# A state-space layer with two layer norms on one core: the states' product goes ahead of the transposes in pass B

## The reference

```python
xn    = layernorm(x) * gamma + beta
delta = sigmoid(xn @ w_delta + b_delta)        # 16 states
B     = xn @ w_in + b_in
gate  = sigmoid(xn @ w_gate + b_gate)          # 512 x 512
h_t   = tanh((h_{t-1} * delta_t) @ A + B_t)    # scan over 2048 tokens
x     = layernorm(x + (h @ C) * gate + x)
x     = layernorm(x + real(ifft(fft(x) @ w)) + bias)   # w complex, 512 x 512
```

## Time and profile before

| | |
|---|---|
| median of 3 executions | 883.58 us |
| the profiled execution | 883.95 us, its span 882.2 us |
| PE busy | 845.7 us, 96% |
| DVE busy | 744.0 us, 84% |
| POOL busy | 573.6 us, 65% |
| ACT busy | 558.6 us, 63% |
| granted TensorE clock | 0.996 of full, mean |

### The profile page before, as it was taken

How to read it: one execution, slowest core, us unless ns; L and a number is a source line. 1 busy time by engine, 2 the same in 40 slices (tenths; PEclk the granted TensorE clock), 3 DMA queues, 4 the chain that set the end, 5 groups by cost and what they waited for, 6 DMA issues and landing times.

```text
span 882.2 us, 16544 instructions
## 1 busy us (share of the span) xinstructions
PE 845.7 (96%) x5062; PEld 453.8 (51%) x5094; DVE 744.0 (84%) x1507; ACT 558.6 (63%) x1060; POOL 573.6 (65%) x906
## 2 busy tenths in 40 slices
PE   8889999999889999999999999999999999999996
PEld 5445445454444555554455555554555555555553
DVE  7788888889999889888789999888888888888883
ACT  5244444544444444454368888888888888888887
POOL 4565566687755465656756767676777777777772
PEclk9999999999999999999999999999999999999999
DMA  8388888777665656877556575767868766866843
GB/s 309 144 288 303 312 303 320 256 262 271 211 220 197 233 183 233 295 243 246 204 175 213 194 237 192 236 223 245 255 239 259 244 234 236 271 221 223 276 152 143
DMA packets 94190, 209.52 MB, mean 238 GB/s; under 512 B 3761, under 2 KB 5041, under 8 KB 90161
## 3 DMA queue, kind: packets, MB, share of 16 engines
q1 hardware_dynamic: 93840, 208.49, 69.0%
q10 hardware_dynamic: 288, 0.27, 0.2%
HBM read 139.53 MB, written 67.11 MB: 234 GB/s over the span
## 4 chain that ended last, share of the span: by engine, by line
PE 56%; DVE 13%; issue 11%; POOL 10%; DMA 5%; ACT 4%; another core or an unknown queue 0%; POOLq 0%; DVEq 0%; SPq 0%; ACTq 0%
PE bank L1508 15%; PE bank L1509 14%; PE bank L1511 14%; PE bank L1479 5%; POOL lo_sb L798 5%; DMA x_sb<-x 5%; DVE bn L1224 3%; PE bank L1664 2%; PE bank L1591 2%; DVE xs_sb L1256 2%; DVE gsum_sb L1271 2%; PE bank L1571 1%; ACT hi_sb L557 1%; DVE zh_sb L1140 1%; DMA w_ring<-w_gate 1%
## 5 line engine op out<-in xcount | busy, mean ns | idle before, releaser
L798 POOL TENSOR_TENSOR lo_sb<-xs_sb,hi_sb 128x512 f16<-128x512 f32 x128 | 150.0, 1172 | 147.1 <-ACT hi_sb L557 147.1
L1508 PE MATMUL bank<-wg_hi,hi_sb 128*128 128x512 f16 x508 | 192.8, 380 | 7.5 <-DVE gsum_sb L1271 6.1
L877 POOL TENSOR_TENSOR x_sb<-x_sb,gate_sb 128x512 f32<-128x512 f32 x120 | 152.9, 1275 | 70.8 <-DMA x_sb<-x 66.6
L1508 PE MATMUL bank<-w_re_sb,hi_sb 128*128 128x512 f16 x512 | 194.0, 379 | 1.5 <-DVE w_ring L1382 1.5
L1509 PE MATMUL bank<-w_re_sb,hi_sb 128*128 128x512 f16 x512 | 194.0, 379 | 0.0
L1509 PE MATMUL bank<-wg_lo,hi_sb 128*128 128x512 f16 x508 | 192.6, 379 | 0.0
L557 ACT ACTIVATE hi_sb<-xs_sb 128x512 f16<-128x512 f32 x128 | 80.5, 629 | 173.5 <-DVE xs_sb L1256 171.1
L1261 DVE SCALAR_TENSOR_TENSOR lo_sb<-bank,hi_sb 128x512 f16<-128x512 f32 x128 | 88.5, 692 | 55.6 <-ACT hi_sb L717 54.0
L1511 PE MATMUL bank<-w_re_sb,lo_sb 128*128 128x512 f16 x512 | 131.4, 379 | 0.0
L1511 PE MATMUL bank<-wg_hi,lo_sb 128*128 128x512 f16 x508 | 131.3, 381 | 0.0
L725 ACT ACTIVATE norm_sb<-x_sb,lift_bias,rstd 128x512 f32<-128x512 f32 x128 | 103.1, 806 | 14.3 <-POOL lift_bias L890 14.1
(11 more groups left out here) (198 smaller groups left out, 1351.7 us busy)
## 6 DMA issues: line engine op xcount, KB each, us to landing
x_sb<-x SPq DMA_DIRECT2D x63, 1024.0 KB, 6.4
gate_dram<-gate_sb SPq DMA_DIRECT2D x32, 1024.0 KB, 5.2
out<-out_sb SPq DMA_DIRECT2D x31, 1024.0 KB, 5.4
gate_sb<-gate_dram SPq DMA_DIRECT2D x30, 1024.0 KB, 7.1
out_sb<-x_turned SPq DMA_DIRECT2D x16, 1024.0 KB, 7.4
norm_sb<-x_turned SPq DMA_DIRECT2D x15, 1024.0 KB, 7.3
w_ring<-gate_dram SPq DMA_DIRECT2D x2, 1024.0 KB, 9.6
x_sb<-x SPq DMA_DIRECT2D x2, 512.0 KB, 6.2
```

The costliest lines, as they stand in the source:

```text
L798: pool.tensor_tensor(lo_sb[:, k % 4], xs_sb[:, k % 2], hi_sb[:, k % 4], ALU.subtract).then_inc(s_lo, 1)
L877: pool.tensor_tensor(x_sb[:, k // 4, k % 4], x_sb[:, k // 4, k % 4], gate_tile(n, k), ALU.add).then_inc(s_v, 1)
L1508: nc.tensor.matmul(dst, hi_sb[:, slot_of, t], w_hi[:, t], start=(t == 0), stop=False)
```

## The change

In `slot_b` of TensorE the states' product of tile n + 7 is issued ahead of the transposes of tile n + 1, behind the scan's step. Nothing else differs.

```diff
             def slot_b(n, k, v):
                 scan_slot(1, n)
+                if exists(n + 7):
+                    states_out(n + 7, (k + 7) % 8, v if k < 1 else v + 1)
                 if exists(n + 1):
                     transpose(n + 1, k + 1, s_bnorm, s_bhi, s_blo, s_bt)
-                if exists(n + 7):
-                    states_out(n + 7, (k + 7) % 8, v if k < 1 else v + 1)
                 if exists(n):
                     ffn(n, k)
                 check_slot(1, n)
```

## The result

The changed kernel takes 888.09 us (median of 6 executions, 886.76 to 889.11), the kernel before 883.66 us (6 executions beside them, 882.09 to 884.31). The ratio is 1.0047, 95% interval 1.0035 to 1.0058: **slower by 4.2 us** (the two medians lie 4.4 apart), where 1.9 were forecast, and outside the range. A second set of 6 gave 1.0040 (1.0025 to 1.0055).

The account below looks back on a forecast made before the run. PE's own instructions were taken to set the pace. Terms 0.6 - 0.5 + 0.7 + 0.5 + 0.5 gave +1.8 us, 1.9 unrounded, so 885.5 us against a median of 883.58; range 882.5 to 887.8.

Parts of the forecast that it names:

- quiet slots keep 3.24 us: Some 85 of 128 slots where nothing waits: PE's own work stays 3.24 us a slot, cost 0.
- new waits for `gated`: Sign: in slots 40, 42, 44 and 46 the states' product newly waits for `gated`.
- `ffn_sum` would cost more: Sign: PE's waits for `ffn_sum` grow from 1.5 us in five places to over 2 in more.
- Both rivals on the low side: Product fills the waits for the normalisation, 882.5 us, chance 0.17; shift taken up everywhere, within 0.5 of 883.6, chance 0.12.
- the ring of 3.24 us: Rival: loop from `gated` through states' product and transposes back becomes the bound, +11, 894 us, chance 0.06.
- the forecast's own case: The summed terms hold: time between 883.8 and 887.4 us, chance 0.65.
- Slot 0, +0.6: Slot 0: twelve products start 0.65 us later, 0.07 comes back in slot 2; bounds 0.5 to 0.7.
- Scan's spacing, -0.5: Slots 5 to 33: transposes' first load is hidden behind the states' product, 0.017 us a slot; bounds -0.5 and 0.
- Scan's VectorE, +0.7: Slots 6, 12 and 20: POOL's residual sums move by 0.22 us, delaying VectorE's product and `ffn_sum`; bounds 0 and 0.9.
- The split, +0.5: Slots 38 to 46: states' high half later, VectorE's low half ends after POOL's sum, which moves 0.22 us; bounds 0.2 and 1.4.
- the bound of 1.4: Upper bound for slots 38 to 46: VectorE's low half keeps its 1.27 us, so four stalls add up.
- Late loads, +0.5: Slots 54 and 122, and 0.1 in slot 58: late x loads make the second wait 0.22 us longer; bounds 0 and 0.8.

Follow-up runs that it names:

- e1: New order in slots up to 4 only, the old one behind, against the kernel before: 1.0015.
- e0: The changed kernel measured once more, against the kernel before: 887.68 us, 1.0040.
- e6: The changed kernel with eight unused 512-column products in slot 0's wait, against the kernel before: 886.87 us, 1.0029.
- e2: New order in slots 5 to 37 only, the old one elsewhere, against the kernel before: 1.0003.
- e5: Old order in slots 0 to 4, new order from slot 5 on, against the kernel before: 885.47 us, 1.0017.
- e9: The changed kernel with the load of x issued ahead of the store of results, against the kernel before: 885.16 us, 1.0016.
- e12: New order from slot 5 on, load of x ahead of the store, against the kernel before: 882.32 us, 0.9994.
- e4: New order from slot 56 on only (hardware loop and end), against the kernel before: 1.0015.
- e13: The changed kernel with slot 0's filler products, four banks for the states' product and x ahead of the store, against the kernel before: 884.86 us, 1.0011.

## Why the prediction was wrong

The direction and most places were right: quiet slots keep 3.24 us, new waits for `gated` stand in slots 40, 42, 44 and 46, slots 38 to 46 and the late loads pay. That `ffn_sum` would cost more was wrong: it vanishes from PE's waits, as `gated` comes first. Both rivals on the low side fell with the interval, which starts at 1.0035; the ring of 3.24 us never closed. The chance for the forecast's own case went to the right mechanism, but +1.9 became +4.2. By its steps:

- **Slot 0, +0.6.** The start was right: 0.61 late, 0.07 back in slot 2. The step that failed is "The transposes fill the wait", followed only to PE's next start. Taking them out made one idle time of 2.21 us out of 1.17 and 0.17, and behind it the granted clock falls to 0.50 in some executions, which costs 1.5 us more each (1.5 in the trace of e1, 1.6 in that of the change again), and 1.5 in the median span (e0 against e6, 0.8 to 3.1). A fall in two executions of three, the estimate above, would be 1.0 in the mean. The bounds of 0.5 to 0.7 left no room for it: the trace of before showed both idle times and no fall, but nothing of what an idle time of 2.2 us does.
- **Scan's spacing, -0.5.** Not there. By the unrounded starts the gap behind the scan's step shrank by 3 to 5 ns a slot, not by 17; in the rows below it is 0.42 us from the first of L1591 (489.87) to the next matmul, and 0.23 from that to the transposes. The bound "the gap stays with the step" was the true value.
- **Scan's VectorE, +0.7.** Not there in slots 6 and 12; slot 20 lost 0.18 (0.2 forecast), and the stretch as a whole nothing. The sum of slot 12 on POOL did not move by 0.22 against PE but by -0.20 (488.12 to 487.03, where slot 12 stands 0.89 earlier). The step "That sum hangs on a load of x, so it moves by 0.22" took a load's time as fixed to 0.1 us; the load issued in slot 9 took 6.80 us before and 6.42 in after. Together the scan cost 0 against +0.2 forecast, measured +0.3 (-0.9 to +1.4) in e2.

```profile
487.03 1.27 POOL L877 TENSOR_TENSOR x_sb<-x_sb,gate_sb 128x512 f32<-128x512 f32 x1
...
487.31 1.24 DVE L1140 TENSOR_TENSOR zh_sb<-h_sb,del_sb 64x128 f32<-64x128 f32 x1 [0.20 <-ACT h_sb L644]
...
489.87 0.59 PE L1591 MATMUL bank<-zh_sb,scan_a 128*128 128x128 f32 x2
...
490.29 0.40 PE L1664 MATMUL bank<-c_parts,h_rep 128*128 128x512 f16 x1
```

- **The split, +0.5.** Right in size with the store first: 0.56 to 0.61 in four traces and 0.84 in one, against 0 to 0.18 in four with the old order there. With x first it does not show: 0.57 and 0.70 against 0.41 and 0.62. VectorE's low half ends 0.55 us after POOL's sum, which is why 0.5 and not 1.4 came out. The case of 1.7 us in the first trace of after is the one where the sum of slot 43 starts 0.19 us ahead of the low half of slot 42. That lies above the bound of 1.4, which knew only a sum that moves by 0.22.
- **Late loads, +0.5.** Undersized. From slot 50 to 127 the trace of after loses 1.7 us, that of the change again 2.1 and e5's 2.2; over all traces the new order loses 1.5 in the mean and the old one 0.55, so about 1.0 is the order's. The step that failed is "So in slots 54 and 122, and 0.1 in slot 58": it took the loads as they were in one execution, and that one had the shortest load of slot 49. The load of the earlier trace rows took 7.54 us to its sum before, 8.25 in after, and with loads of 6.2 to 6.6 us in slot 49 the same slots cost 0.14 us (e9) or gain 0.5 (e12), against a gain of 0.75 under the old order. The spare of the twelve products fell as forecast (unrounded 0.48 before and 0.26 after, 0.15 needed). That this is what lets longer loads be charged is argued, not shown: the load of slot 49 is charged under both orders.

So of +4.2 us, by spans: 0.6 for slot 0's start and 1.5 for the clock behind it (e6 against e5 and the change), 1.2 (e5 against before) for the split and the loads. They make up the 3.35 by which the median span of the change stood above before's beside them. By the traces the split and the loads are more, 0.5 and 1.0. The yardstick itself moves by that much: the median span of the kernel before was 882.50 us in this set and 881.50 to 881.70 in the three others, and against those e5 stands 2.0 to 2.2 higher and the change 4.2 to 4.4. So the shares are good to about 1 us. Open are the +1.3 us that e4 measured, where its trace (the fastest of its executions) shows 0.6, and the rest of e13.

## What to carry to other kernels

Before an instruction leaves a wait that it used to fill, add up the idle time on TensorE on both sides of it, not only the start of what comes next: here two short waits that became one of 2.2 us brought the clock down in some executions, and each fall cost 1.5 us in the matmuls behind, on top of the wait. A change that only eats spare costs what varies: look at how far the loads scatter from execution to execution and compare the remaining spare with that, not with one trace. One trace of the kernel before is one draw too. And where a load is late, look which transfers stand around it in its queue; here a load and a store swapped gave 0.14 to 0.18%.

## What the runs showed of the hardware

- PE's granted clock fell to 0.50 of full (1.2 GHz) at the end of one idle time of 2.22 us in two of six traces, and in none of the nine with 1.17 and 0.17 us nor in the two that had eight products in the wait. In e1 it was back from 449 us on (0.99 from 449 to 451 us), 3 us behind the end of the idle time.
- The load of 1 MB of x in slot 49 lands in 6.2 to 6.6 us with the store issued 0.42 us behind it (five traces) and in 7.4 to 8.1 us with the store issued about 2 us ahead of it (twelve), with four transfers of the states behind in both. From slot 57 on, without those, it is 6.4 and 6.3 us in the mean.
- The two kernels with eight more matmuls in slot 0 had 2.6 and 2.8 us outside of the span (medians of 12 and 11 executions), all others 1.8. What this is, the profile does not show; an added filler is to be judged by the span as well as by the time.
- VectorE's low half of the states (0.69 us alone), when it started during POOL's sum, ended 0.55 us after the sum's end, in 35 places of 17 traces. A sum that started during the low half ended 1.13 us after its end. In slot 42 the sum started 190 ns ahead of the low half in one trace and 19 ns or more behind it in the sixteen others.
